# Cross-attention with two masks on other engines, weighted values in two runs instead of three, and the query projection one slot later

## The reference

```python
# query: 32 x 112 x 256 (layer-normed x), key = value = ctx: 32 x 375 x 256, 16 heads of 16
Q, K, V = split(query @ wq.T), split(key @ wk.T), split(value @ wv.T)
scores = einsum('bhqd,bhkd->bhqk', Q, K) / sqrt(16)
scores = where(mask == 1, -1e9, scores)
attn = softmax(scores)
out = einsum('bhqk,bhkd->bhqd', attn, V)        # heads put together again
return out @ w_out.T
```

## Time and profile before

| | us |
|---|---|
| median of 3 runs | 1335.5 (1333.16 to 1335.74) |
| the profiled execution | 1333.69 |
| its span | 1331.9 |

### The profile page before, as it was taken

How to read it: one execution, slowest core, us unless ns; L and a number is a source line. 1 busy time by engine, 2 the same in 40 slices (tenths; PEclk the granted TensorE clock), 3 DMA queues, 4 the chain that set the end, 5 groups by cost and what they waited for, 6 DMA issues and landing times.

```text
span 1331.9 us, 34415 instructions
## 1 busy us (share of the span) xinstructions
PE 1223.9 (92%) x10866; PEld 1105.3 (83%) x10866; DVE 900.2 (68%) x2932; ACT 762.9 (57%) x1780; POOL 502.6 (38%) x709
## 2 busy tenths in 40 slices
PE   4899999999998788999999999999999887999994
PEld 4789989889887777888888888889888776888884
DVE  4685674855846456778778877777887575655548
ACT  3543344343343317788888888888888853555530
POOL 2242241322321332344444444444444451333335
PEclk9999999999999888899999999999999898999997
DMA  8499800000000235465666665556566143333358
GB/s 205 113 221 227 188 0 0 0 0 0 0 0 23 67 97 123 126 153 142 151 150 149 152 149 145 142 141 155 141 158 153 47 142 89 104 101 101 105 141 246
DMA packets 131263, 151.39 MB, mean 114 GB/s; under 512 B 41107, under 2 KB 111108, under 8 KB 131156
## 3 DMA queue, kind: packets, MB, share of 16 engines
q1 hardware_dynamic: 124436, 134.55, 42.1%
q0 software_dynamic: 6160, 15.69, 3.5%
q10 hardware_dynamic: 576, 0.07, 0.0%
HBM read 79.27 MB, written 45.82 MB: 94 GB/s over the span
## 4 chain that ended last, share of the span: by engine, by line
PE 47%; ACT 5%; DVE 4%; issue 3%; DMA 2%; POOL 2%; SPq 1%; ACTq 0%; DVEq 0%; POOLq 0%
PE psum L875 8%; PE psum L1161 6%; PE psum L1147 6%; PE psum L1124 6%; PE psum L1296 6%; PE psum L1316 3%; ACT pr L1653 2%; PE psum L1142 2%; PE psum L1093 2%; PE psum L1189 2%; ACT psum L1662 1%; PE psum L1339 1%; PE psum L1208 1%; DVE x_res L2331 1%; PE psum L1287 1%
## 5 line engine op out<-in xcount | busy, mean ns | idle before, releaser
L2194 DVE CUSTOM_DVE_ANT_0 junk<-psum,biasq 112x375 f32<-112x375 f32 x512 | 267.0, 541 | 102.1 <-issue 66.1
L1653 ACT ACTIVATE pr<-psum 125x448 f32<-125x448 f32 x384 | 203.7, 539 | 29.6 <-PE psum L1147 27.9
L1147 PE MATMUL psum<-qst,kst 97*125 97x224 f32 x768 | 198.0, 318 | 10.5 <-ACT psum L1662 10.0
L1124 PE MATMUL psum<-kst,qst 96*112 96x376 f32 x512 | 167.7, 354 | 3.0 <-DVE smax L2194 2.9
L1147 PEld LDWEIGHTS psum<-qst,kst 97*125 97x125 f32 x768 | 141.6, 192 | 27.3 <-ACT psum L1662 26.2
L1662 ACT ACTIVATE psum<-flagk 125x448 f32<-125x448 bf16 x256 | 140.7, 550 | 7.6
L717 POOL TENSOR_TENSOR rs<-rs,neg_half 112x1 f32<-112x1 f32 x32 | 18.2, 570 | 248.7 <-DVE rs L2107 248.7
L841 POOL DMA_INDIRECT routed_y<-yb,yrow x61 | 58.8, 964 | 123.5 <-ACT yb L1841 120.9
L1124 PEld LDWEIGHTS psum<-kst,qst 96*112 96x112 f32 x512 | 90.2, 181 | 11.1 <-DVE smax L2194 8.2
L1161 PE MATMUL psum<-pr,vaug 125*32 125x112 f32 x3072 | 96.6, 268 | 0.0
L759 POOL DMA_INDIRECT routed_h<-h,slot x64 | 78.2, 1223 | 32.4 <-POOL h L748 14.7
(11 more groups left out here) (320 smaller groups left out, 3525.0 us busy)
## 6 DMA issues: line engine op xcount, KB each, us to landing
kst<-khi SPq DMA_DIRECT2D x64, 376.0 KB, 4.5
routed_h<-in_route_pad SPq DMA_DIRECT2D x6, 3640.0 KB
kst<-klo SPq DMA_DIRECT2D x32, 376.0 KB, 6.1
ctxT<-in_ctxT SPq DMA_DIRECT2D x32, 375.0 KB, 3.5
hblk<-routed_h SPq DMA_DIRECT2D x61, 130.0 KB, 2.1
qst<-qhi SPq DMA_DIRECT2D x128, 56.0 KB, 2.4
stage<-in_e SPq DMA_DIRECT2D x21, 256.0 KB, 3.4
maskq<-in_mask SPq DMA_DIRECT2D x32, 164.1 KB
```

The lines of the kernel that those rows point to most:

```text
L1124: pe.matmul(bank[max_bank(n, par, hd)][0:T, 0:S2E], head(qst[par][0:ROWS], hd), pair(kst[par][0:ROWS], hd // 2), start=True, stop=True).th ...
L1147: mm = pe.matmul(bank[q % 2][0:KP, cols(i, 2 * T)], pair(kst[par], n)[:, cols(q // HPB, KP)], both(qst[par], n), start=False, stop=True, s ...
L1653: nc.scalar.activation(pr[q % PROBS][:].rearrange("k i q -> k (i q)"), bank[q % 2][0:KP, 0:GT], ACT.Exp, scale=1.0 / HD ** 0.5).then_inc(s ...
L2194: nc.vector.tensor_tensor_reduce(out=junk[:, hd % 2, :], in0=bank[max_bank(n, par, hd)][0:T, 0:S2], in1=biasq[:, par, :], scale=1.0, scala ...
```

## The change

Masks: `WRITTEN` becomes 2, 3, 4, 6, 7, 8, 9, 10. So the mask of slot 5 is made by TensorE and that of slot 10 by ScalarE. Weighted values: two runs of six slots, in slot 7 (slots 0 to 5) and in slot 1 of the next row (slots 6 to 11). For that there are 8 `pr` buffers: slots 0 to 7 have one each, and 8 to 11 use those of 2 to 5. The waits of the exponentials follow. The query projection and `transpose_on` go to slot 6, with their copies on ScalarE, and change their order; `qlo` on VectorE goes from slot 6 to slot 7. The last third of V's projection goes from slot 8 to slot 9 and its copy from ahead of exponential 9 to ahead of exponential 10. `biasq` and `junk` (the maxima's discarded output) become bf16.

```diff
-PROBS = 6
+PROBS = 8
+PENDING = 6
-WRITTEN = range(2, 10)
+WRITTEN = (2, 3, 4, 6, 7, 8, 9, 10)
-            biasq = w2("biasq", [T, RB, S2])
+            biasq = w2("biasq", [T, RB, S2], BF16)
-            junk = w2("junk", [T, 2, S2])
+            junk = w2("junk", [T, 2, S2], BF16)
+        def probs(q):
+
+            return q if q < PROBS else q - PENDING
# TensorE, step
-                    if q % HPB == 1 and q > HPB:
-                        for earlier in range(q - HPB - 1, q - 1):
+                    if q == PENDING + 1:
+                        for earlier in range(PENDING):
                             weighted_values(t, par, earlier)
                     elif q == 1 and not first:
-                        for earlier in range(SLOTS - HPB, SLOTS):
+                        for earlier in range(PENDING, SLOTS):
                             weighted_values(*prev, earlier)
...
-                    if q == 5 and following >= 2:
+                    if q == 6 and not first:
+                        transpose_on(*prev)
+                    if q == 6 and following >= 2:
                         project_q(*far)
-                    if q == 5 and not first:
-                        transpose_on(*prev)
...
                     if q == 8 and following >= 2:
                         project_v(*far, 1)
+                    if q == 9 and following >= 2:
                         project_v(*far, 2)
# ScalarE, exponentials and step
-                act.wait_ge(s2["pv_done"], done + 1)
+                if q % PENDING >= PROBS - PENDING:
+                    act.wait_ge(s2["pv_done"], done + 1)
+                elif not is_row(t * RB + par, 0):
+                    act.wait_ge(s2["pv_done"], done + 1 - PENDING)
...
-                    if q == 9 and following >= 2:
+                    if q == 10 and following >= 2:
                         copy_v(*far, 1)
                     exponentials(t, par, q)
...
-                    if q + 2 in WRITTEN:
+                    if q + 2 in WRITTEN and q < 8:
                         write_mask(t, par, q + 2)
...
+                    if q == 6 and not first:
+                        copy_on(*prev)
+                    if q == 6 and following >= 2:
                         high_q(*far)
-                    if q == 5 and not first:
-                        copy_on(*prev)
                     if q == 8 and following >= 1:
                         negate_max(*nxt)
+                    if q == 8:
+                        write_mask(t, par, 10)
# VectorE, step
-                            if q == 6 and following >= 2:
+                            if q == 7 and following >= 2:
                                 low_q(*far)
```

More of the change, by code:

```diff
@@ L1065, in _ @@
             pe.wait_ge(s["w_in2"], 16 * 2)
-            pe.nop().then_inc(s2["pv_done"], PROBS)
+            pe.nop().then_inc(s2["pv_done"], PENDING)
             def project_k(t, par, m):
@@ L1137, in mask_scores @@
                 if q in WRITTEN:
-                    pe.wait_ge(s["cmask"], G * len(LEVELS) + len(WRITTEN) * b + q - WRITTEN[0] + 1)
+                    pe.wait_ge(s["cmask"], G * len(LEVELS) + len(WRITTEN) * b + WRITTEN.index(q) + 1)
                     return
@@ L1160, in weighted_values @@
                     row = 2 * HD * i
-                    mm = pe.matmul(bank[6][row:row + 2 * HD, cols(hd // HPB)], vaug[par][:, c3, hd], pr[q % PROBS][:, i],
+                    mm = pe.matmul(bank[6][row:row + 2 * HD, cols(hd // HPB)], vaug[par][:, c3, hd], pr[probs(q)][:, i],
                                    start=q == 0, stop=c3 == KC - 1, skip_group_check=True)
@@ L1444, in _ @@
             step(ROUNDS + 1, 1, following=0)
-            for q in range(SLOTS - HPB, SLOTS):
+            for q in range(PENDING, SLOTS):
                 weighted_values(ROUNDS + 1, 1, q)
@@ L1651, in exponentials @@
                 act.wait_ge(s2["sc_ps"], done + 1)
-                act.wait_ge(s2["pv_done"], done + 1)
-                nc.scalar.activation(pr[q % PROBS][:].rearrange("k i q -> k (i q)"), bank[q % 2][0:KP, 0:GT], ACT.Exp, scale=1.0 / HD ** 0.5).then_inc(s2["exp"], 1)
+                if q % PENDING >= PROBS - PENDING:
+                    act.wait_ge(s2["pv_done"], done + 1)
+                elif not is_row(t * RB + par, 0):
+                    act.wait_ge(s2["pv_done"], done + 1 - PENDING)
+                nc.scalar.activation(pr[probs(q)][:].rearrange("k i q -> k (i q)"), bank[q % 2][0:KP, 0:GT], ACT.Exp, scale=1.0 / HD ** 0.5).then_inc(s2["exp"], 1)
             def write_mask(t, par, q):
@@ L1665, in copy_pv @@
                 p = t * RB + par
-                act.wait_ge(s2["pv_done"], SLOTS * (p + 1) + PROBS)
+                act.wait_ge(s2["pv_done"], SLOTS * (p + 1) + PENDING)
                 nc.scalar.copy(pv[:], bank[6][:, 0:GT]).then_inc(s2["pv_sb"], 1)
```

## The result

| | before | after |
|---|---|---|
| median, us | 1334.35 (4 runs, 1333.16 to 1335.74) | 1353.48 (4 runs, 1350.42 to 1357.43) |
| ratio | | 1.0145 (1.0115 to 1.0174) |
| the profiled execution, us | 1333.69 | 1350.42 |
| 27 rows, us | 472.39, 17.50 a row | 491.17, 18.19 a row |

What follows compares the result with a forecast made beforehand. TensorE works nearly without a gap, but after the change waits for VectorE at head 13. Stretches 4.33 + 5.15 + 8.34 = 17.82 us against 17.48; +0.30 taken over 27 rows, +8.1 us, gives 1343.5 us, range 1328 to 1351.

Steps and rivals of the forecast that it cites:

- Stretch 1: Row start to head 5's maxima product in slot 2: 3.96 us plus 0.37 for the 24-head run, 4.33 us.
- stretch 2: Head 5 to head 13 (first of slot 6): 5.15 us, as head 13 waits for head 10's maximum on VectorE.
- stretch 3: Head 13's maxima product to the next row's start: 6.97 us before, summed at 8.34 us after the change.
- Last third of V to slot 9, its copy ahead of exponential 10: ... Nothing: V's last projection third: the same products, moved behind the scores, so counted at no cost.
- ScalarE isn't late for anything that decides, so I count this at nothing: ScalarE's 0.97 us wait for the query projection, moved to slot 6, mostly goes; counted as no gain.
- less the run of 16 in slot 9 (0.90): Head 13 to next row: removing slot 9's run of 16 heads' weighted values saves TensorE 0.90 us.
- The slack shrinks from 1.0 to 0.4 us but holds: Row end, SyncE's queue: negated maxima land at 786.5, ahead of the next row's mask product due at 786.89.
- A: Rival, faster: bf16 operands shorten VectorE's maxima by 0.20 us each, row 17.23 us, 1328.5 us; chance 0.18.
- C: Rival, slower: later `qhi` makes SyncE's negated maxima land late; 2.7 us per further 0.1 us, 1352 with 0.3; chance 0.12.
- D: Rival: a run of 24 costs 1.5 us with its entry, 7 us more over 27 rows, 1350.5 us; chance 0.05.

## Why the prediction was wrong

**Right.** The direction, and the step that carried it. Stretch 1 was summed at 4.33 us and is 4.32; stretch 2 at 5.15 and is 5.16; a run of 24 at 1.27 and takes 1.28 (786.97 to 788.25); behind the wait the next product comes 0.26 us later, as taken from the earlier trace rows. VectorE's chain from head 5 to head 10 kept its length: head 10's maximum is out 5.10 us behind TensorE's head 5 (779.71 to 784.81), 5.09 in the earlier trace rows.

**Wrong, stretch 3.** It was summed at 8.34 us and takes 8.54. The step that failed is "Last third of V to slot 9, its copy ahead of exponential 10: ... Nothing", together with "ScalarE isn't late for anything that decides, so I count this at nothing". With it went the term "less the run of 16 in slot 9 (0.90)", which took that run out as if nothing stood under it. I had counted what is moved on TensorE and had not followed ScalarE's queue past slot 8. Without the run of weighted values in slot 9, the end of V's second third, ScalarE's copy, exponential 9 and mask 11 stand in one line: ScalarE's exponential 9 runs until 792.34 and mask 11 starts at 792.40.

```profile
791.31 0.58 ACT L1647 COPY vaug<-psum 125x512 f32<-125x512 f32 x1 [0.20 <-PE psum L880]
791.79 0.55 ACT L1662 ACTIVATE pr<-psum 125x448 f32<-125x448 f32 x1
```

That is 0.14 us ahead of the mask and 0.06 in its own slot (0.46 for 0.40), 0.20 a row and 27 x 0.20 = 5.4 us; the other terms of the stretch are off by up to 0.1 us each way and cancel. The kernel before had the same chain with 0.9 us of products inside it. The experiments bear it out from three sides: with exponential 9 ahead of the copy mask 11 is 0.22 us behind the scores, with the run back in slot 9 it is 0.21 and takes 0.41, and in the kernel with the two runs alone, with V's last third in slot 8 and the old masks, the wait is larger, 0.40. So it is the run taken away that opened the wait; that V's last third in slot 9 covers a part of it again is likely and not shown by itself.

**Wrong, the slack of the transfers.** "The slack shrinks from 1.0 to 0.4 us but holds" is true of the regular row: the negated maxima are issued at 790.97, land 1.8 us later at 792.77, and their mask starts at 793.41, 0.64 later. But I reckoned it for the negated maxima alone, and `qlo` has less, 0.36 us. It was put as a rival for a lasting delay. What came is an issue or a landing that is a microsecond late once in some rows; the kernel before has it too and has the slack for it. The irregular part is 491.2 - 487.4 = 3.8 us in the 27 rows, a part of it with a landing as the named cause; the cause of the rest is open.

**The size.** I took +0.30 a row from a sum of 0.25 to 0.34. Regular rows are +0.57, the mean +0.69. Of the 0.39 that was missed, 0.20 is ScalarE's end of the row, some 0.14 the irregular rows, and the rest my choice below the upper sum. The rest of the kernel gave 2.1 us back, which I had put at nothing, 1.5 to either side.

**The rivals.** A is settled against by the run with bf16 alone and by the 543 ns. The Trainium skill, VectorE: DVE Perf Modes, section The perf-mode tier table, gives `tensor_tensor` with a PSUM operand the plain rate, and the trace agrees for this operation, a custom one (541 ns with float32, 543 with bf16). C named the right queue and had the wrong form, a constant shift. D is settled against by the 1.28 us. The range ended at 1351 because C and D were priced one at a time; ScalarE's queue at the row's end was in no rival at all.

**And the change as a whole.** The sum counted 0.27 us for the merged runs and 0.39 for the masks as gains of one package. Taken apart, the masks give 11 us (1332.7 to 1321.7); the moves of the query projection and V's last third, put on top with bf16 and the buffers, take 12 to 16 (12.1 by the 27 rows, 1321.7 to 1337.8 in all); the two runs, on top of these, take another 13 to 16 (12.7 by the 27 rows, 1337.8 to 1353.5 in all). On the kernel before the two runs alone take 34. So with masks and moves in place the two runs cost less than half, and the moves cost about as much themselves. Which of the two moves costs it, and what the masks have in the halving, no run separates.

## What to carry to other kernels

A block of work that nobody waits for is cover: ahead of removing, merging or moving it, list every round trip that it lies inside (TensorE to another engine and back), and sum each with the block gone, for every engine's queue to the end of the loop. A fixed cost of 0.27 us was saved here, and the two round trips that the removed runs had covered were worth 0.8 and 0.4 us by starts. When one change consists of several edits, price and run them alone: here one of them is a gain by itself, and it is the one to keep. An experiment that moves work on the engine that is waited for is stronger than one that moves the waiter, because it leaves the waiter's order as it was.

## What was not expected of the hardware

In this kernel an issue by SyncE to the query stacks takes 0.59 us as a rule, but single ones take up to 1.77 us (the four of `qhi` at 568.09 took 3.47 us together), and a landing of the negated maxima comes 1.8 us behind its issue as a rule and once 3.5. The kernel before shows the same, up to 1.77 and 2.9 us. So a slack below a microsecond on these transfers is not a slack in every row. And taking a mask product away from behind a run of weighted values leaves some of its cost there: the two scores behind the run take 0.31 us, and 0.21 elsewhere. In the kernel with three runs V's product behind the run of slot 9 is dearer by the same 0.1 us (0.34, 785.66 to 786.00, where 0.24 is usual).
